# Expert sublayers of a decoder: token results gathered two chunks ahead into three buffers, in place of one chunk ahead into two

## The reference, cut to what matters

```python
x = _layernorm(x + _L0_attn_ref(...))   # 8 experts, top 2:  moe_first
...
x = _layernorm(x + _L1_ffn_ref(...))    # 32 experts, top 1: L_ffn (moe_small)
...
x = _layernorm(x + _L3_ffn_ref(...))    # 8 experts, top 1, with a capacity: moe_last

# L3_ffn, as an example
logits = xf @ wg
scores = softmax(logits)
top1 = argmax(scores)
slot = top1 * capacity + rank           # place of the token in its expert's rows
eb[slot] = xf
h = gelu(einsum('ecd,edf->ecf', eb, W1) + b1)
y = einsum('ecf,efd->ecd', h, W2) + b2
out = y[slot] * combine_w               # the gather that this case is about
```

## Time and profile before

| what | value |
|---|---|
| time, median of 3 runs | 3843.98 us (3837.57 to 3857.55) |
| the profiled execution's own time | 3835.76 us |
| its span, first to last instruction | 3834.1 us |
| mean granted tensor clock | 0.877 |
| busy: PE, DVE, POOL, ACT | 77%, 57%, 47%, 46% |
| token_y gathers, moe_first, L_ffn, moe_last | 128, 64, 64 |
| one gather on POOL | 0.94 to 1.16 us, median 0.945 |
| expert weights, tile rows in and out (8 experts) | 578, 128 and 128 KB a tile |

### The profile page before, as it was taken

The page is one execution under the profiler, slowest core; times in us unless marked ns, Lnnn a source line. Parts: engine busy times, 40 slices in busy tenths (PEclk is TensorE's granted clock), DMA queues, the critical chain, the costliest instruction groups (busy, mean ns, idle before and its releaser), DMA issues. The chain is left out here.

```text
span 3834.1 us, 81924 instructions
## 1 busy us (share of the span) xinstructions
PE 2937.7 (77%) x28058; PEld 2008.0 (52%) x28058; DVE 2196.2 (57%) x6036; ACT 1775.5 (46%) x3334; POOL 1808.2 (47%) x1671
## 2 busy tenths in 40 slices
PE   3298853788888789963539997997999778996792
PEld 3277752565555556652316664663444435665672
DVE  2001323755888668862348886776776496884033
ACT  0143421434555556621216665775565546661341
POOL 1643435324776745526465545661222445553444
PEclk9999986999999899975559998997998699996896
DMA  6376631020001121214611112220000002221673
GB/s 228 95 230 183 193 118 56 23 7 18 35 36 41 42 72 69 73 40 126 164 50 46 55 53 90 88 86 28 1 1 1 4 1 72 73 66 59 192 223 95
DMA packets 310160, 300.23 MB, mean 78 GB/s; under 512 B 108516, under 2 KB 231942, under 8 KB 309769
## 3 DMA queue, kind: packets, MB, share of 16 engines
q1 hardware_dynamic: 271208, 249.89, 21.3%
q0 software_dynamic: 16384, 33.59, 2.9%
q10 hardware_dynamic: 22304, 13.39, 1.2%
HBM read 157.03 MB, written 55.84 MB: 56 GB/s over the span
## 5 line engine op out<-in xcount | busy, mean ns | idle before, releaser
L832 DVE TENSOR_TENSOR moe_first_tile_y<-moe_first_out_ps,moe_first_expert_w 128x256 f32<-128x256 f32 x78 | 33.1, 424 | 368.1 <-PE moe_first_out_ps L968 313.1
L1009 ACT ACTIVATE moe_first_hid<-moe_first_hid_ps,moe_first_expert_w 128x256 f32<-128x256 f32 x312 | 128.0, 471 | 191.1 <-PE moe_first_hid_ps L957 150.6
L1029 POOL DMA_INDIRECT slot_x<-x_tok,moe_first_slots x128 | 123.8, 967 | 179.3 <-DVE moe_first_tile_y L832 75.2
L968 PE MATMUL moe_first_out_ps<-moe_first_expert_w,moe_first_hid 128*128 128x128 f32 x1248 | 177.3, 294 | 20.6 <-ACT moe_first_hid L1009 16.7
L968 PEld LDWEIGHTS moe_first_out_ps<-moe_first_expert_w,moe_first_hid 128*128 128x128 f32 x1248 | 161.8, 200 | 30.4 <-DVE moe_first_tile_y L832 15.0
L1043 POOL DMA_INDIRECT moe_first_token_y<-slot_y,moe_first_slots x128 | 123.9, 968 | 98.7 <-issue 64.4
L1708 POOL TENSOR_TENSOR causal_k_blocks<-causal_k_T,headmask 128x1024 f32<-128x1024 f32 x64 | 121.3, 1897 | 99.7 <-PE causal_scores L1318 94.0
L1708 POOL TENSOR_TENSOR alibi_k_blocks<-alibi_k_T,headmask 128x1024 f32<-128x1024 f32 x64 | 121.3, 1898 | 94.1 <-PE alibi_scores L1318 90.0
L2871 PE MATMUL L_ffn_experts<-weights_odd,x_T 128*128 128x512 f32 x256 | 163.4, 724 | 2.0 <-ACT L_ffn_expert_out L2968 1.8
L1708 POOL TENSOR_TENSOR full_k_blocks<-full_k_T,headmask 128x1024 f32<-128x1024 f32 x64 | 120.8, 1898 | 85.0 <-PE full_scores L1318 80.0
L957 PE MATMUL moe_first_hid_ps<-moe_first_tile_xT,moe_first_expert_w 128*128 128x256 f32 x624 | 154.2, 392 | 0.9 <-issue 0.9
(11 more groups left out here) (548 smaller groups left out, 8965.1 us busy)
## 6 DMA issues: line engine op xcount, KB each, us to landing
moe_first_expert_w<-in_L_attn_experts SPq DMA_DIRECT2D x78, 578.0 KB
moe_last_expert_w<-in_L_ffn_experts SPq DMA_DIRECT2D x46, 578.0 KB
slot_x<-blank ACTq DMA_DIRECT2D x2, 4992.0 KB, 45.3
moe_first_tile_x<-slot_x SPq DMA_DIRECT2D x78, 128.0 KB
slot_y<-moe_first_tile_y SPq DMA_DIRECT2D x78, 128.0 KB
L_ffn_tile_x<-slot_x SPq DMA_DIRECT2D x32, 256.0 KB
slot_y<-L_ffn_tile_y SPq DMA_DIRECT2D x32, 256.0 KB
moe_last_tile_x<-slot_x SPq DMA_DIRECT2D x46, 128.0 KB
```

Of the source, the lines that this page charges most:

```text
L832: dve.tensor_tensor(y_out[:, q, :, :], out_bank[q][:, 0:SLOT_TILE].rearrange("p (s d) -> p s d", s=SPAN), over(wall[:, j % RING, 2 * FF + ...
L968: last = pe.matmul(out_bank[j % 2][:, D * s:D * s + D], hid[:, j % 2, b, TILE * s:TILE * s + TILE], wall[:, j % RING, FF + D * b:FF + D * ...
L1009: act.activation(hid[:, j % 2, b, :], hid_bank[b // 2][:, SLOT_TILE * (b % 2):SLOT_TILE * (b % 2) + SLOT_TILE], gelu, bias=wall[:, j % RIN ...
L1029: pool.indirect_dma_start(slot_x[part][:, :], bass.IndirectOffsetOnAxis(slots[:, part, r, t:t + 1], 0), net.x_tok[:, part * K + t, :], Non ...
```

## The change

`y_in` gets a third buffer in all three sublayers, with a semaphore each, and chunk c uses buffer c mod 3. `gather(c)` waits for the combine of chunk c - 3 in place of c - 2. In GpSimd's list each part now begins with the gathers of three chunks, and ahead of chunk c's inverse standard deviation stands the gather of chunk c + 2 where that of c + 1 stood; the last two chunks of a part have no gather ahead of theirs. The residual sums and the statistics keep two buffers. VectorE's list keeps its order.

```diff
-    RING, XRING = 4, 3
+    RING, XRING, YRING = 4, 3, 3
...
-        y_in = sb("token_y", [128, 2, PER, top, D])
+        y_in = sb("token_y", [128, YRING, PER, top, D])
...
-        gathered = [sem("token_y_landed_even"), sem("token_y_landed_odd")]
+        gathered = [sem(f"token_y_landed{n}") for n in range(YRING)]
...
                 def combine(c):
-                    p, part = c % 2, c // PC
-                    dve.wait_ge(gathered[p], 16 * PER * top * (c // 2 + 1))
+                    p, q, part = c % 2, c % YRING, c // PC
+                    dve.wait_ge(gathered[q], 16 * PER * top * (c // YRING + 1))
...
                 def gather(c):
-                    p, part = c % 2, c // PC
+                    p, part = c % YRING, c // PC
                     if c % PC == 0:
                         for q in range(2):
                             pool.wait_ge(y_stored[q], 16 * (((part + 1) * NT + 1 - q) // 2))
-                    if c >= 2:
-                        pool.wait_ge(tail.summed, c - 1)
+                    if c >= YRING:
+                        pool.wait_ge(tail.summed, c - YRING + 1)
...
                 for c in range(CHUNKS):
                     if c % PC == 0:
                         gather(c)
-                    if (c + 1) % PC:
                         gather(c + 1)
+                    if c % PC + 2 < PC:
+                        gather(c + 2)
                     tail.inverse_std(pool, c)
```

More of the change, by code:

```diff
@@ L846, in combine @@
                             base_row = net.x_tok[:, PER * c + k, :] if r == 0 else tail.r[:, p, k, :]
-                            last = dve.scalar_tensor_tensor(tail.r[:, p, k, :], y_in[:, p, k, r, :], weights[:, part, r, t:t + 1],
+                            last = dve.scalar_tensor_tensor(tail.r[:, p, k, :], y_in[:, q, k, r, :], weights[:, part, r, t:t + 1],
                                                             base_row, ALU.mult, ALU.add)
@@ L2300, in moe_small @@
     slot_x, slot_y = dram["slot_x"], dram["slot_y"]
-    RING, XRING = 4, 6
+    RING, XRING, YRING = 4, 6, 3
     sub = Sublayer(net, name)
@@ L2330, in moe_small @@
         y_out = sb("tile_y", [128, 2, 4, D])
[L2331 removed]
+        y_in = sb("token_y", [128, YRING, PER, D])
         tail = RowTail(sub, final)
@@ L2421, in combine @@
                 def combine(c):
-                    p = c % 2
-                    dve.wait_ge(gathered[p], 16 * PER * (c // 2 + 1))
+                    p, q = c % 2, c % YRING
+                    dve.wait_ge(gathered[q], 16 * PER * (c // YRING + 1))
                     if c >= 2:
                         dve.wait_ge(tail.normed, c - 1)
-                    dve.scalar_tensor_tensor(tail.r[:, p, :, :], y_in[:, p, :, :], 0.0, net.x_tok[:, chunk_tiles(c), :],
+                    dve.scalar_tensor_tensor(tail.r[:, p, :, :], y_in[:, q, :, :], 0.0, net.x_tok[:, chunk_tiles(c), :],
                                              ALU.max, ALU.add).then_inc(tail.summed, 1)
```

## The result

| | before | after |
|---|---|---|
| median, beside each other | 3843.72 us (20 runs) | 3855.52 us (20 runs) |
| profiled execution | 3835.76 us | 3847.92 us |
| granted tensor clock | 0.877 | 0.877 |

The ratio is 1.003, 95% interval 1.0018 to 1.0043: 11.8 us slower (6.9 to 16.5), within the 0.5% that the prediction called no change. It had said 3852 us and +8.2.

A forecast was written before the change was run, and what follows sets the result against it. The tail was taken as bound by POOL's gather issue, the middle's tiles as held up by gather bursts. Terms 5.1 + 2.6 + 2.3 - 1.8 = +8.2 us gave 3852 us, +0.2%, range 3838 to 3863.

The forecast's parts named there:

- The bound of the tail: Tails after part two's last tile: bound by POOL's issue of 64 gathers, not by how far ahead they run.
- Rival C: Tails: the gathers' landing was on their path, so clearly faster, -41 us, 3803 us; chance 0.02.
- moe_first's middle, +5.1: First burst grows from 16 to 24 gathers, +9.3, less 4.2 for the 8-burst that goes; bounds -4.2 and +10.0.
- L_ffn, +2.6: Its middle: first burst grows from 8 to 12 gathers, +3.6, less 1.0 for the burst that goes; bounds -1.0 and +5.0.
- moe_last, +2.3: Its middle: first burst grows from 8 to 12 gathers, +3.6, less 1.25 for the burst that goes; bounds -1.25 and +5.0.
- The tails, -0.6 each: End of each tail: last gathers finish 1.45 us earlier, last combine starts 0.6 us earlier; -1.8 us in all three.
- I0 behind G2, 0: Middle: chunk 0's inverse standard deviation behind chunk 2's gathers on POOL delays nothing; 0, at most 1 us each.
- Buffers and semaphores, 0: Each sublayer: a third buffer and third semaphore add no instruction except what the barrier clears; taken as 0.
- DVE's wait for gathered rows still near 60 us: A sign in the tail: DVE's waits for gathered rows, 62.3 us before, would hardly change.
- Rival B: Middle: a burst's cost doesn't grow with its length; -1.8 to -8.2 us, 3836 to 3842 us; chance 0.28.
- Rival D: Boundaries between parts: tiles stand for the whole longer burst and the clock falls behind it; +20 us, 3864 us; chance 0.08.
- The rule weighed: Middle: DMA engines take turns between queues, so an unchanged number of gathers costs 0 there; sum -1.8 us.

The follow-up runs named there:

- plain_rows: Changed kernel with each gather by index replaced by a plain DMA of 128 consecutive rows (wrong rows, times the issue only); one execution, 3701.97 us.
- tail_two_ahead: Changed kernel with three buffers, but the middle's gathers one chunk ahead as before, only the tails two ahead; 3788.08 us, ratio 0.9999 to the kernel before.
- before_again: The kernel before, unedited, profiled again beside the others of a later group on one chip; 3838.84 us profiled.
- middle_two_ahead: Changed kernel with the middle's gathers two chunks ahead, but the tails one ahead as before; 3800.20 us, ratio 1.003 to the kernel before.
- after_again: The changed kernel, unedited, timed and profiled again beside the others of a later group; 3858.71 us, ratio 1.0035 to the kernel before.
- std_early_again: Changed kernel with chunk 0's inverse standard deviation ahead of chunk 2's gathers on POOL, on a chip without stalls; 3792.75 us, ratio 1.0017 to the kernel before.
- second pair: The kernel before and the changed kernel, both unedited, run again beside each other on one chip that stalls; ratio 1.0035.
- second group: Later runs on one chip: both kernels again, an early first inverse standard deviation, and three chunks ahead in the middle; kernel before 3841.94 us.

## Why the prediction was right, step by step

- **The bound of the tail: right.** The gathers stay 1.25 us apart in the tails, the lookahead changed no tail by more than 2 us, and a shorter issue took 93.5 us off the three (plain_rows). Rival C (-41 us) fell with tail_two_ahead.
- **moe_first's middle, +5.1: right in mechanism, small in size.** +6.4 and +8.0 in the two pairs. Going from 16 to 24 gathers cost the wait 11.1 us in both pairs (26.31 - 15.16, 25.60 - 14.47), where the term taken was 8 x 1.16 = 9.3. That slope was measured between 8 and 16 and was too flat: a burst of 8 costs 4.2 us, half of what POOL takes to issue it, while beyond 16 each gather costs 1.40.
- **L_ffn, +2.6: mis-sized.** +5.5 and +6.7, beyond the upper bound of 5.0. The term that was mis-sized is the slope, 0.9 us a gather: four more gathers put the second eviction behind the first gather off by 5.6 us in both pairs (11.58 to 17.19, 11.61 to 17.21), 1.40 each. The bound took POOL's 1.25 for the most that a gather can cost. After, the timeline has two long waits there, where before the second was 2.40 and 3.80 us:

```profile
1862.46 0.69 DVE L2420 COPY L_ffn_tile_y<-L_ffn_out_ps 128x512 f32<-128x512 f32 x1 [10.24 <-DMA slot_y<-moe_first_tile_y]
1872.55 0.69 DVE L2420 COPY L_ffn_tile_y<-L_ffn_out_ps 128x512 f32<-128x512 f32 x1 [9.40 <-DMA slot_y<-moe_first_tile_y]
```

  (The releaser named is a store of moe_first, whose last eviction was at 542.5 us; what ended these waits the profile doesn't say.)
- **moe_last, +2.3:** +5.9 and +2.1. The term can't be called wrong or right from two executions of each: its reading of +3.6 for four gathers stands against +4.5 and +2.8 from the first gather to the second eviction behind it.
- **The tails, -0.6 each: right in moe_first and moe_last, not shown in L_ffn** (-1.0, +1.8, -0.3; then -0.7, -0.2, -0.6). L_ffn's tail of before alone is 57.4 in one execution and 59.4 in another. In moe_first the last combine starts 91.31, 91.06 and 90.90 us behind the tail's first gather with one chunk ahead (before, before_again, middle_two_ahead), and 90.21 to 90.42 with two (after, after_again, tail_two_ahead, std_early_again).
- **I0 behind G2, 0: right on the chips that stall, wrong as a general statement.** This step of the prediction failed. The working rested on C0 being late because the tiles stall. Where they don't, C0 comes during the burst, and the same edit costs +8.0 and +3.7 through N0. The prediction took a property of one chip's trace for one of the kernel.
- **Buffers and semaphores, 0: right** (tail_two_ahead, 0.9999).
- **"DVE's wait for gathered rows still near 60 us": wrong.** It fell to 21.3. The term "what is late next is N13" was right and should have been applied to every chunk of the tail, not the last alone.
- **Rival B** (the burst's cost doesn't grow) is refuted where bursts cost anything, by 14.47, 25.60, 36.07. **Rival D** (+20) was near in the second pair, +16.8. It needed that nothing be won back by the burst that goes; in moe_first 3 to 5 of the added 11.1 us were.
- **The sum, +8.2** against +11.8 (6.9 to 16.5) and, in the second pair, +16.8 (8.1 to 19.2). It was low because two slopes were too flat; with 1.40 in each sublayer the same sum is 22.4 - 6.4 - 1.8 = +14, an estimate between the two measured. On a chip without stalls the forecast of +8.2 would have stood near the truth by luck alone: middle_two_ahead costs 13.9 us there, through N0's wait and not through the mechanism that was forecast.

**The rule weighed.** The Trainium skill, "DMA: Bandwidth & Descriptors", section "Queues, rings and completion order", has the engines take turns between queues with work. DMA queues of after, 344 to 368 us, in the stall:

```profile
q0 software_dynamic: 577, 1.18, 17.9%
q1 hardware_dynamic: 433, 0.73, 10.5%
```

and of tail_two_ahead, 338 to 357 us, inside its burst:

```profile
q1 hardware_dynamic: 2832, 3.79, 65.6%
q0 software_dynamic: 416, 0.85, 16.9%
```

(packets, MB, share of 16 engines). Without stalls the trace agrees with the rule: gathers and loads share, and the four beats of the tiles inside the burst are 4.04, 5.21, 4.04 and 4.07 us. On the stalling chip the queues are simply not asked: from 340 to 372 us SP has one wait, 24.4 us, for the eviction whose result it is to store, and its loads stand behind that. The result of -1.8 that the rule gave was wrong on both kinds: on the one DMA has room while the tiles stand, and on the other the cost comes from DVE's wait for POOL.

**What the stall is stays open.** It is seen in two traces of before, in the first of after, and in every trace of the second group; it begins and grows with POOL's back-to-back issue and ends, in moe_first, 2.9 to 5.2 us behind it. In after_again PE's last record ends at 358.69, from 362 to 368 us only POOL is busy (the second fence: PE, PEld, DVE, ACT, POOL, clock, DMA), and ACT starts again at 371.58, 0.12 us behind DVE's eviction at 371.46:

```profile
358.31 0.38 PE L946 MATMUL moe_first_turn_ps<-ident,moe_first_tile_x 128*128 128x128 f32 x2
```

```profile
362.00:368.00 6.00, 0.00 (x0) 0.00 (x0) 0.00 (x0) 0.00 (x0) 4.13 (x5) 0.56 0.17 46
```

```profile
356.02 0.38 ACT L1000 ACTIVATE moe_first_tile_xT<-moe_first_turn_ps 128x256 f32<-128x256 f32 x1 [2.67 <-remote]
371.58 1.57 ACT L1009 ACTIVATE moe_first_hid<-moe_first_hid_ps,moe_first_expert_w 128x256 f32<-128x256 f32 x4 [15.18 <-remote]
```

Both wait for PE by the program, and 4.1 us lie between the last gather's end (367.34) and DVE. Either PE's work ended later than its records say, or its signal was late, or the waiting engines started late though released. The Trainium skill, "Perfetto Trace Analysis", section "Summary: the profiler window per engine type", calls TensorE's recorded end an estimate and leaves the signal's travel out of the record, so the trace can't tell the first two apart. For the third speak two rows of the same burst, in which ACT and PE stand 4 us each and the profile shows nothing that they waited for:

```profile
352.51 0.84 ACT L1009 ACTIVATE moe_first_hid<-moe_first_hid_ps,moe_first_expert_w 128x256 f32<-128x256 f32 x2 [4.04 <-issue]
353.04 2.93 PE L968 MATMUL moe_first_out_ps<-moe_first_expert_w,moe_first_hid 128*128 128x128 f32 x12 [4.02 <-issue]
```

In tail_two_ahead's burst (338 to 357 us) no engine but POOL has such a wait. "Issue" can hide a wait, though, as in the tail above. No run here separates the three.

## What to carry to other kernels

A longer lookahead on an in-order queue also pushes back everything that stands behind it: before adding a chunk to a burst, name the small operation behind the burst and the engine that waits for it. Keeping it in front gave moe_first's middle 7 us back where bursts stop nothing (178.0 to 171.1, in two traces), and nothing where the burst itself stops the tiles. A large wait that the change names is worth its size only if the engine it waits for is not itself the bound; the tail lost 41 us of waits for rows and 1 us of time. And compare stage lengths only between traces of one chip: a gap of 31 us between two chips looked like the success of an edit.

## What was not expected of the hardware

- The kernel before has two levels of time, further apart than any two kernels here that give the right result on one chip. It took 3843.72 and 3841.94 us in the first comparison and the second group, and 3786.27, 3787.66 and 3788.80 in three others, 55 us or 1.5% less. These three were three different chips and the second group a fourth; each was used once, so that it is the chip that differs, and not something else about those runs, is likely and not shown. Take the profiled executions of before_again and tail_two_ahead, whose middle is the same: they are 42.8 us apart, and their middles sum to 378.8 and 340.2 us, so 38.6 of it lie in the stages where POOL issues gathers while tiles run; another 8.3 lie in L_ffn's tiles before its first gather (79.3 for 71.0).
- The mean granted clock hardly differs: 0.877 and 0.879 in these two executions, and 0.876 against 0.880 or 0.881 as the middle value of the runs of before.
- POOL takes 0.944 us for an indirect gather of 128 rows, with 0.30 behind it, and 0.544 with nothing behind it for a plain DMA of as many bytes.
- Where bursts stall the tiles, the tiles come back at 1.40 us for each gather of the burst, slower than POOL issues them (1.25), in moe_first and in L_ffn alike.
